# A causal-attention stage on one core: row items mixed in width and head, with a new table of places

## What is computed

```python
q = _apply_rope(split_heads(xn @ W_q), cos, sin)
k = _apply_rope(split_heads(xn @ W_k), cos, sin)
scores = jnp.einsum('bhqd,bhkd->bhqk', q, k)
scores = jnp.where(causal, -jnp.inf, scores)
attn = jax.nn.softmax(scores / jnp.sqrt(jnp.float32(hd)), axis=-1)
ctx = jnp.einsum('bhqk,bhkd->bhqd', attn, v)
```

## Time and profile before

| | us |
|---|---|
| median of 3 runs | 2648.99 |
| lowest, highest | 2640.83, 2650.19 |
| profiled execution, its own time | 2668.93 |
| its span | 2667.2 |

### The profile page before, as it was taken

The page is one execution under the profiler, slowest core; times in us unless marked ns, Lnnn a source line. Parts: engine busy times, 40 slices in busy tenths (PEclk is TensorE's granted clock), DMA queues, the critical chain, the costliest instruction groups (busy, mean ns, idle before and its releaser), DMA issues. The chain is left out here.

```text
span 2667.2 us, 53565 instructions
## 1 busy us (share of the span) xinstructions
PE 2530.6 (95%) x16876; PEld 1274.2 (48%) x16877; DVE 2136.1 (80%) x6183; ACT 1782.9 (67%) x4187; POOL 988.9 (37%) x1187
## 2 busy tenths in 40 slices
PE   7999993999999999999999999999999999899777
PEld 6878781333333333333333333333333333588666
DVE  7888886888888888888888888888888888354344
ACT  5777770677777777777777777777777777655111
POOL 6888884222222222222222222222222222222665
PEclk9999995999999999999999999999999999999888
DMA  7999998446556456455457465455464561597997
GB/s 240 351 347 354 353 328 194 103 96 112 106 99 113 94 100 116 97 103 115 89 106 151 88 108 110 89 111 114 90 116 100 93 111 38 170 310 274 299 320 218
DMA packets 305865, 435.04 MB, mean 163 GB/s; under 512 B 101808, under 2 KB 204464, under 8 KB 305584
## 3 DMA queue, kind: packets, MB, share of 16 engines
q1 hardware_dynamic: 293296, 398.05, 58.1%
q0 software_dynamic: 12288, 33.57, 5.6%
HBM read 241.18 MB, written 188.74 MB: 161 GB/s over the span
## 5 line engine op out<-in xcount | busy, mean ns | idle before, releaser
L884 DVE CUSTOM_DVE_ANT_0 dump<-ps_rows,mask 128x512 bf16<-128x512 f32 (+7 forms) x2048 | 1481.2, 754 | 224.4 <-issue 185.4
L863 ACT ACTIVATE probs<-ps_cols 128x512 f32<-128x512 f32 (+3 forms) x3072 | 1315.8, 495 | 514.5 <-PE ps_cols L1032 503.9
L1032 PE MATMUL ps_cols<-q_st,k_st 99*128 99x512 bf16 (+3 forms) x3072 | 863.3, 329 | 5.5 <-DMA q_st<-max_T 3.3
L842 POOL TENSOR_SCALAR_AFFINE_SELECT probs<-probs 128x512 f32<-128x512 f32 x512 | 325.9, 636 | 1363.8 <-ACT probs L863 1363.8
L976 PE MATMUL ps_rows<-k_st,q_st 96*128 96x512 bf16 (+3 forms) x3072 | 781.7, 331 | 29.5 <-DMA v_st<-v_dram 21.9
L1008 PE MATMUL ps_ctx<-probs,v_st 128*32 128x512 f32 (+3 forms) x6144 | 655.2, 498 | 1.5 <-POOL probs L842 1.3
L1032 PEld LDWEIGHTS ps_cols<-q_st,k_st 99*128 99x128 bf16 x3072 | 279.8, 97 | 591.0 <-ACT probs L863 380.8
L976 PEld LDWEIGHTS ps_rows<-k_st,q_st 96*128 96x128 bf16 x3072 | 265.3, 98 | 326.5 <-DVE row_max L884 127.8
L1008 PEld LDWEIGHTS ps_ctx<-probs,v_st 128*32 128x32 f32 x6144 | 120.9, 108 | 206.5 <-issue 103.3
L280 POOL TENSOR_TENSOR roped<-rope_c,rope_s 128x512 f32<-128x512 f32 x128 | 165.0, 1289 | 41.0 <-DVE rope_s L404 40.8
L884 DVE DVE_READ_ACCUMULATOR2_ANT row_max<- 128x1 f32 x2048 | 168.7, 82 | 0.2
(11 more groups left out here) (113 smaller groups left out, 2669.6 us busy)
## 6 DMA issues: line engine op xcount, KB each, us to landing
parts_dram<-parts SPq DMA_DIRECT2D x128, 384.0 KB, 3.8
q_st<-parts_dram SPq DMA_DIRECT2D x384, 128.0 KB
k_st<-parts_dram SPq DMA_DIRECT2D x384, 128.0 KB
v_dram<-v_sb SPq DMA_DIRECT2D x128, 256.0 KB, 5.2
v_st<-v_dram SPq DMA_DIRECT2D x64, 512.0 KB
xs_dram<-zeros SPq DMA_DIRECT2D x36, 512.0 KB, 6.9
xs_sb<-xs_dram SPq DMA_DIRECT2D x72, 256.0 KB, 4.9
g_dram<-g_sb SPq DMA_DIRECT2D x72, 256.0 KB, 3.5
```

Of the source, the lines that this page charges most:

```text
L842: nc.gpsimd.affine_select(out=tri, in_=tri, compare_op=ALU.is_ge, fill=0.0, base=0, pattern=[[0, GH], [1, P]], channel_multiplier=-1).then ...
L863: nc.scalar.activation(probs[:, k % PB, h, 0:w], ps_cols[(GH * k + h) % CB][:, 0:w], ACT.Exp).then_inc(exp_done, 1)
L884: nc.vector.tensor_tensor_reduce(out=dump[:, even, 0:n], in0=ps_rows[:, 512 * bank:512 * bank + n], in1=mask[:, S - n:S], scale=1.0, scala ...
L1032: nc.tensor.matmul(ps_cols[(GH * k + h) % CB][:, 0:w], k_st[r][:, j // IB, h * 512 + (j % IB) * P:h * 512 + (j % IB + 1) * P], q_st[r][:, ...
```

## The change

`ITEMS` becomes a written list, in which each half's 16 items stand mixed in width and head, and `ORDER` is another table. Half 0 still comes ahead of half 1, the same 32 items and 12 values, two M and two X are there, and every instruction keeps its shape. Banks, slots and distances follow from the two tables through `place()`. Lines behind the tables move down by 3.

```diff
-    ITEMS = [(i, h) for c in range(HALVES) for i in range(IB * (c + 1) - 1, IB * c - 1, -1) for h in range(GH)]
+    ITEMS = [(0, 0), (0, 2), (2, 2), (0, 1), (2, 1), (1, 2), (3, 2), (3, 3),
+             (3, 1), (1, 3), (1, 1), (0, 3), (2, 0), (1, 0), (3, 0), (2, 3),
+             (7, 3), (4, 1), (7, 0), (7, 1), (7, 2), (6, 3), (6, 1), (6, 0),
+             (4, 0), (4, 2), (5, 2), (6, 2), (5, 0), (5, 3), (5, 1), (4, 3)]
     ORDER = (
-        ("R", "R", "R", "RRV"),
-        ("R", "R", "V", "R"),
...
+        ("RR", "R", "RR", "RV"),
+        ("", "MRR", "RR", "V"),
+        ("", "R", "RX", "RR"),
+        ("", "RV", "R", "R"),
+        ("", "", "RVV", ""),
...
```

More of the change, by code:

```diff
@@ L634, in attention_phase @@
     ORDER = (
-        ("R", "R", "R", "RRV"),
-        ("R", "R", "V", "R"),
[L637 to L646, removed]
+        ("RR", "R", "RR", "RV"),
[3 more added lines that the diff above has]
+        ("", "", "RVV", ""),
+        ("RR", "V", "", "R"),
+        ("R", "", "VR", ""),
+        ("", "MX", "R", ""),
+        ("R", "V", "R", "R"),
+        ("", "V", "R", ""),
+        ("R", "V", "R", "R"),
+        ("V", "", "R", "V"),
     )
```

## The result

The change is faster than forecast. The runs of the changed kernel have a median of 2608.48 us (2604.66 to 2609.07) beside 2645.89 for the kernel before: a ratio of 0.9856, 95% interval 0.9833 to 0.9879, or 37 us less. The forecast was 2622, its range 2611 to 2638. The time lies under the range.

What follows compares the result with a forecast made beforehand. TensorE was taken as the bound, at 28.38 us a group. Per group −0.10 (entries) −0.38 (old waits) +0.04 (new waits) = −0.44; 63 groups give −28, +1 once: 2649 − 27 = 2622 us, range 2611 to 2638.

Steps and rivals of the forecast that it cites:

- Entries: Per group, 14 entries from the bfloat16 stream into V, M or X instead of 15: −0.10 us (0.09 in, 0.01 out).
- The four waits: Waits behind M (0.23), ahead of V(0) (0.06), X (0.04) and at half 1's head (0.05) go: −0.38 us a group.
- The collision: Group head: VectorE's L904, held by a GpSimd select, loses 0.43 us; TensorE waits of 0.23 and 0.04 go with it.
- New waits: Eight places where TensorE arrives under 0.1 us after what it needs: +0.04 us a group, bounds 0 to 0.30.
- (c): V(4) waits for ScalarE's copy of half 0: TensorE's cover 1.63 us, before 2.3; ScalarE needs 1.2 to 1.8.
- (a): Slot 4 wants slot 0's bank: TensorE is there at 1.01 us, VectorE lets go at 0.91; slack 0.10.
- (b): Behind M and X at step 7, the second wide item wants X's bank: TensorE 1.71 us, VectorE 1.70; level.
- The rate and the total: Attention: −0.44 us a group over 63 groups, 28 us; with +1 once only, −27 us in all.
- The collision stays: Rival, 0.05: at the group head L904 comes a microsecond later, is held again; group gains 0.11, 7 us, time 2642.
- Half: Rival, 0.12: wide half's level places pay 0.2 more, or V behind V drains and (c) pays its upper end; 2634 us.
- Nothing: Rival, 0.05: the old waits of 0.38 just move to (a) to (c); time within 5 us of 2649.
- Slower: Rival, 0.08: VectorE-to-TensorE handovers at eight banks take longer; at 0.15 more each, the group is 0.37 longer, 2672 us.

Runs made afterwards that it cites:

- e1: Kernel before with split_max of half 1 one slot later, so L904 falls behind the select, both tables untouched; 2625.35 us, ratio 0.9924.
- control: The changed kernel run again unchanged, beside the kernel before; 2603.08 us, ratio 0.9837, and on a further occasion 2603.66, ratio 0.9840.
- Pair b: Changed kernel with both tables rewritten: three pairs of neighbouring V, V(0) behind the first M, X ahead of M at step 9; 2837.22 us, ratio 1.0656.

## Why the prediction was right or wrong

**The place and the causes were right, two sizes were not.** TensorE was the bound, by entries and waits, and a group is what they change.

The sum missed 0.30 us a group: about half of it at the entries and half at the old waits.

- *Entries, forecast 0.10, measured 0.24.* **This is the step that failed by its reasoning.** I took the way back from a V as 0.01, since the row behind a V is only that much longer. But the way out is inside V's own row. The rows of after give it: V of 128 columns 0.35 (1446.01 to 1446.36), of 256 0.57 (1471.49 to 1472.06), of 512 0.99 (1448.17 to 1449.16). That is 0.213 for each 128 columns and a fixed 0.14. The pair has 384 columns: 3 · 0.213 + 0.14 = 0.78, and took 0.79. The 0.14 is paid once. The trace of before had V's of all four widths too; I had priced one. The Trainium skill, "TensorEngine Tiling (Array Packing)", section "Key Properties", says that a change of tiling mode drains TensorE, with no figure. The trace agrees, at 0.10 in and 0.14 out. By the same rule X, which uses the whole array, should pay nothing, and pays nothing (1449.62 to 1449.68); my "each entry into V, M or X" was wrong for X. M, with 48 columns of weights, pays as V does: 0.10 ahead of it (1446.36 to 1446.80, 0.44 for 2 · 0.17), and 0.17 for itself (1446.80 to 1446.97) where an item of 128 columns takes 0.06. So what pays is what uses a part of the array's columns, 32 or 48; that M changes the tiling mode too is not shown.
- *The four waits, forecast 0.38, measured about 0.54.* The collision alone is 0.36 (e1) where I had 0.27: what I booked at X as an entry of 0.09 was for the most part a wait, and X ran 0.06 longer behind it. **This is the other half of what failed: a wait counted as an entry.** The wait ahead of V(0) is 0.09 once the collision is gone (e1), that at the head of half 1 0.05, and one of 0.04 stands in e1 ahead of a block at step 2.
- *New waits, forecast +0.04, measured +0.05.* (c) pays 0.04. (a) and (b) hold.
- Together 0.24 + 0.54 − 0.05 = 0.73, and 0.74 was seen; 0.01 is left over.
- *The rate and the total.* 63 · 0.69 (the mean over all groups) = 44; control against before, each pair on one chip, gave 42.0 and 42.3, the first result 37.4. What is missing may lie behind attention, where single executions spread by more than that. The 20 us between the profiled execution and the median did stay out of it: 376.6 us of the profile of before lie behind attention, some 20 more than in most others, with late signals behind the gathers.

*The rivals.* "The collision stays" is refuted by L907's 0.17. "Half" counted on V behind V draining all the same; it does not. "Nothing" fell as well. "Slower" came true in one set of runs, but by another mechanism than the one that I described: not by handovers at eight banks, but by one late signal of 0.9 at (c). Its price of 23 us and the 20 us seen agree by chance.

*The range.* It was built from the bounds of the waits and from the spread of the runs. The term with no bound was the entry, as I thought that I had measured it.

## What to carry to other kernels

When a kind of instruction comes in several sizes, fit its duration against its size: here the constant (0.14) was the cost of leaving it, while the cost of coming to it (0.10) stood in the row ahead, and the two together tell what putting two side by side saves. A wait for a late engine can sit inside the duration of what waits (X, 0.06 longer) and inside what looks like a fixed cost, so compare the same instruction at two places before calling a difference a cost. And cover that is cut from 0.7 us to nothing still costs nothing in a clean run; it is the reserve against a signal that comes late, so a gain of this sort is to be measured on more than one occasion. Pair b adds that an account of an order has to name every wait, those for transfers too: 1.98 us a group went to one that its expectation left out.

## What the hardware showed that I had not expected

- TensorE's signals arrived up to 1.1 us late just behind GpSimd's indirect transfers, in one set of runs and in the first profile of before, and cost this order 0.86 a group: 2681.40 instead of 2603.08 us, in the profiles 57 us in attention and 17 behind it (371.3 us from the last column block, instead of 354.0).
- One VectorE operation of 16 elements, held by a GpSimd select, cost 0.36 us of TensorE's time a group, 21 us in all.
- An X whose weights wait for a signal takes 0.49 to 0.50 instead of 0.44.
- One wait of 1.98 us a group (pair b) is followed by 3.4 us or more at 1.2 GHz in every group.
